# A four-layer graph network kernel: work of the last node stage moved between SP, DVE, ACT and POOL

## The reference

```python
x = _layernorm(x + _L2_gnn_ref(x, ...), axis=-1)
x = _layernorm(x + _L3_gnn_ref(x, ...), axis=-1)   # the last layer
...
# inside _L3_gnn_ref, xs and xv the scalar and vector parts of x:
ssa, sva = fctp_scalar_attr(xs, xv, node_attr, Ws_sc_a, Wv_sc_a)
ssc, svc = fctp_scalar_attr(xs, xv, node_crystal_attr, Ws_sc_c, Wv_sc_c)
s_s, s_v = (ssa + ssc, sva + svc)
...
out_s = C_S * s_s + C_X * o_s      # o_s, o_v: the summed messages, mapped
out_v = C_S * s_v + C_X * o_v
```

## Time and profile before

| what | value |
|---|---|
| median of 3 runs | 3911.85 us (3908.62 to 3913.18) |
| the profiled execution's own time | 3914.43 us |
| its span | 3912.6 us |
| busy share of the span | PE 89%, DVE 69%, ACT 56%, POOL 64% |
| mean granted PE clock | 0.967 of full speed |

### The profile page before, as it was taken

One profiled execution on the slowest core, in us unless ns is written; L12 is line 12 of the kernel. 1 busy time (PEld: TensorE's weight loads), 2 busy tenths in 40 slices (PEclk: granted clock), 3 DMA queues, 4 the chain that ended last, 5 costly groups with the idle time before them and its releaser, 6 DMA issues.

```text
span 3912.6 us, 103757 instructions
## 1 busy us (share of the span) xinstructions
PE 3477.1 (89%) x26652; PEld 3218.3 (82%) x26652; DVE 2710.7 (69%) x10501; ACT 2205.7 (56%) x6014; POOL 2489.7 (64%) x2969
## 2 busy tenths in 40 slices
PE   2799998666599999999979999999989999988886
PEld 2799997565499999877779999877779999987775
DVE  3577775888766666588856666588866666657776
ACT  0244443666544444477745555577756666657777
POOL 1477776888667777566667777400046666658887
PEclk9899998888799999999989999999989999999999
DMA  8622223777522222499822222388832222237775
GB/s 353 248 63 62 61 53 101 255 253 258 180 58 59 57 56 50 118 303 299 287 76 63 61 59 55 93 293 298 297 97 55 53 52 50 45 99 243 239 246 199
DMA packets 424012, 572.02 MB, mean 146 GB/s; under 512 B 218794, under 2 KB 242344, under 8 KB 419590
## 3 DMA queue, kind: packets, MB, share of 16 engines
q1 hardware_dynamic: 280742, 289.28, 25.3%
q10 hardware_dynamic: 61488, 166.57, 10.9%
q0 software_dynamic: 81680, 114.98, 10.8%
HBM read 356.01 MB, written 233.79 MB: 151 GB/s over the span
## 4 chain that ended last, share of the span: by engine, by line
PE 59%; ACT 11%; issue 10%; DVE 7%; DMA 5%; POOL 4%; ACTq 2%; DVEq 1%; POOLq 0%; SPq 0%
PE bank L771 17%; PE bank L804 13%; ACT arena L1049 6%; PE bank L814 5%; PE bank L761 4%; PE bank L827 3%; PE bank L824 3%; PE bank L778 3%; PE bank L819 3%; PE bank L796 3%; ACT same_all L1037 2%; POOL mark_ring L638 2%; DVE stats L1380 2%; ACTq L1020 2%; DVE arena L1373 2%
## 5 line engine op out<-in xcount | busy, mean ns | idle before, releaser
L558 POOL DMA_INDIRECT aggregates<-arena,meta x784 | 790.7, 1008 | 459.7 <-issue 252.1
L771 PE MATMUL bank<-same_all,msg 128*98 (+1 forms) x6272 | 758.6, 275 | 0.0
L545 POOL DMA_INDIRECT xg<-x_after,meta x588 | 585.8, 996 | 252.1 <-issue 247.4
L771 PEld LDWEIGHTS bank<-same_all,msg 128*98 128x98 f32 x6272 | 715.8, 167 | 0.1
L1049 ACT ACTIVATE arena<-arena,shift,rstd 128x160 f32<-128x160 f32 x1500 | 658.4, 513 | 64.1 <-DVE shift L1315 61.5
L961 ACT ACTIVATE w<-bank 1x162 f32<-1x162 f32 (+1 forms) x784 | 257.8, 329 | 741.5 <-PE bank L804 737.6
L804 PE MATMUL bank<-w,arena 98*128 98x32 f32 (+1 forms) x4704 | 628.3, 270 | 0.0
L804 PEld LDWEIGHTS bank<-w,arena 98*128 98x128 f32 x4704 | 590.1, 193 | 0.0
L1380 DVE BATCH_NORM_STATS2 stats<-arena 128x6 f32<-128x160 f32 x1600 | 454.3, 313 | 42.9 <-DVE arena L1373 8.9
L1024 ACT ACTIVATE nT<-bank 128x640 f32<-128x640 f32 x400 | 281.8, 705 | 330.3 <-PE bank L883 179.6
L1268 DVE TENSOR_TENSOR arena<-bank,yv 128x192 f32<-128x192 f32 x294 | 105.1, 358 | 477.9 <-PE bank L824 294.2
(11 more groups left out here) (156 smaller groups left out, 7264.2 us busy)
## 6 DMA issues: line engine op xcount, KB each, us to landing
arena<-aggregates SPq DMA_DIRECT2D x400, 324.0 KB, 4.1
x_after<-arena ACTq DMA_DIRECT2D x300, 320.0 KB, 3.9
arena<-x_after SPq DMA_DIRECT2D x300, 320.0 KB, 3.6
aggregates<-arena ACTq DMA_DIRECT2D x25, 1296.0 KB, 14.7
arena<-nodes SPq DMA_DIRECT2D x100, 320.0 KB, 3.9
out<-arena ACTq DMA_DIRECT2D x100, 320.0 KB, 3.8
same_all<-sorted_dst SPq DMA_DIRECT2D x7, 1792.0 KB, 10.9
aggregates<-arena,meta POOLq DMA_INDIRECT x784, 2.3
```

The source lines that it names most:

```text
L545: gp.indirect_dma_start(xg[:, k % XGR, 4 + t * F:4 + (t + 1) * F], None, xtab[l], at).then_inc(gathered[k], 16)
L558: gp.indirect_dma_start(agg, at, tot[:, kk % TRING, t, 0:AW], None, bounds_check=NP - 1, oob_is_err=False).then_inc(spread[kk], 16)
L771: last = nc.tensor.matmul(bank[5 + t][0:MR, c * P:(c + 1) * P], msg[:, k2, t, c, :], same_all[:, bass.ds(here[t], P)], start=True, stop=True)
```

## The change

All of it is in the node stage of the last layer.

1. The stores of the output leave ACT's list. SP issues them (new L491 in the new file), in iteration b for block b-7 (`OUT_LAG = 7`), ahead of the load of x for block b; SP's iterations run on to 106.
2. DVE's `products` gets a fifth STT: row tile 2, g = 0. It waits for the second `sc_ready` of the block and raises `half_done`.
3. ACT makes three gated halves in place of four: (g, j) = (0, 3), (1, 3), and then (1, 2), the last only once `half_done` says that DVE's fifth STT of the block is done. `half_done` counts three to a block where it counted two.
4. POOL's first addition covers row tile 3 alone (160 columns in place of 320). Its normalization of row tile 3 is gone, and so is the semaphore `last_normed`; ACT normalizes all four row tiles.

```diff
@@ sp: node_loads
+                    if l == 3 and within(b, OUT_LAG, NBLK + OUT_LAG):
+                        kk, tt = back(k, turn, OUT_LAG, NRING)
+                        done = b - OUT_LAG
+                        if not isinstance(b, int):
+                            done = sp.snap(done)
+                        sp.wait_ge(normed, node_count(l, b - OUT_LAG))
+                        alone(sp, passed["sp"])
+                        sp.dma_start(out_rows[bass.ds(done, 1)].rearrange("o p c -> (o p) c"), xn[:, place(kk)]).then_inc(stored[kk], 16)
+                    if not within(b, 0, NBLK):
+                        return
                     if not isinstance(b, int) or b >= X_EARLY:
                         wait(sp, stored[k], node_slot(l, k, turn - 1) * 16)
@@ gpsimd: add_both
-                    if within(b, APPLY_LAG[3], NBLK + APPLY_LAG[3]):
-                        gp.wait_ge(shift_ready, b + (1 - APPLY_LAG[3] + l * NBLK))
-                        alone(gp, passed["gp"])
-                        row = xn[:, place(ka), 3 * F:4 * F]
-                        gp.tensor_scalar(row, row, rstd[:, ka, 3:4], shift[:, ka, 3:4], ALU.mult, ALU.add).then_inc(last_normed, 1)
...
-                        gp.tensor_tensor(x, x, second[:, kk % XGR, 0:2], ALU.add).then_inc(first_added, 1)
+                        gp.tensor_tensor(x[:, 3], x[:, 3], second[:, kk % XGR, 1], ALU.add).then_inc(first_added, 1)
                         gp.wait_ge(first_added, b)
                         alone(gp, passed["gp"])
-                        gp.tensor_tensor(x, x, second[:, kk % XGR, 2:4], ALU.add).then_inc(second_added, 1)
+                        gp.tensor_tensor(x[:, 2:4], x[:, 2:4], second[:, kk % XGR, 2:4], ALU.add).then_inc(second_added, 1)
@@ scalar: node_copies
-                    if within(b, STORE_LAG[l], NBLK + STORE_LAG[l]):
+                    if l < 3 and within(b, STORE_LAG[l], NBLK + STORE_LAG[l]):
...
-                        for g in range(2):
-                            for j in (2, 3):
-                                last = nc.scalar.activation(second[:, kk % XGR, 2 * g + j - 2, :], bank[4 + j][:, g * F:(g + 1) * F],
-                                                            ACT.Copy, scale=attr[:, kk, j, g:g + 1])
+                        for g, j in ((0, 3), (1, 3), (1, 2)):
+                            if j == 2:
+                                act.wait_ge(half_done, b * 3)
+                            last = nc.scalar.activation(second[:, kk % XGR, 2 * g + j - 2, :], bank[4 + j][:, g * F:(g + 1) * F],
+                                                        ACT.Copy, scale=attr[:, kk, j, g:g + 1])
                         last.then_inc(second_gated, 1)
...
-                        for t in range(BT - (l == 3)):
+                        for t in range(BT):
@@ vector: products
+                            dve.wait_ge(sc_ready, base + 2)
+                            row = xn[:, place(k), 2 * F:3 * F]
+                            stt(out=row, in0=bank[6][:, 0:F], scalar=attr[:, k, 2, 0:1], in1=row,
+                                op0=ALU.mult, op1=ALU.add).then_inc(half_done, 1)
                             return
```

More of the change, by code:

```diff
@@ L39 @@
 X_EARLY = 4
+OUT_LAG = 7
 XGR = 4
@@ L331, in build @@
         tot_ready, carried, tot_out = sems("tot_ready", 2), sems("carried", 2), sem("tot_out")
-        last_normed = sem("last_normed")
         half_done = sem("half_done")
@@ L451, in _ @@
                 arows = agg.rearrange("(b p t) c -> b p (t c)", p=P, t=BT)
+                out_rows = out.rearrange("(b p t) c -> b p (t c)", p=P, t=BT)
                 def row_load(b, k):
@@ L488, in node_loads @@
                         aggregate_load(b + A_LEAD[l], (k + A_LEAD[l]) % NRING)
-                steps(sp, 0, NBLK, NODE_STEADY if l else LOADS_STEADY, node_loads, NRING)
+                steps(sp, 0, NBLK + (OUT_LAG if l == 3 else 0), NODE_STEADY if l else LOADS_STEADY, node_loads, NRING)
             for k in range(NRING):
@@ L670, in add_both @@
                     kk, tt = back(k, turn, 1, NRING)
-                    ka, ta = back(k, turn, APPLY_LAG[3], NRING)
-                    if within(b, APPLY_LAG[3], NBLK + APPLY_LAG[3]):
-                        gp.wait_ge(shift_ready, b + (1 - APPLY_LAG[3] + l * NBLK))
-                        alone(gp, passed["gp"])
-                        row = xn[:, place(ka), 3 * F:4 * F]
-                        gp.tensor_scalar(row, row, rstd[:, ka, 3:4], shift[:, ka, 3:4], ALU.mult, ALU.add).then_inc(last_normed, 1)
                     if within(b, 0, NBLK):
@@ L686, in add_both @@
                         alone(gp, passed["gp"])
-                        x = xn[:, place(kk)].rearrange("p (t c) -> p t c", t=BT)[:, 2:4]
-                        gp.tensor_tensor(x, x, second[:, kk % XGR, 0:2], ALU.add).then_inc(first_added, 1)
+                        x = xn[:, place(kk)].rearrange("p (t c) -> p t c", t=BT)
+                        gp.tensor_tensor(x[:, 3], x[:, 3], second[:, kk % XGR, 1], ALU.add).then_inc(first_added, 1)
                         gp.wait_ge(first_added, b)
                         alone(gp, passed["gp"])
-                        gp.tensor_tensor(x, x, second[:, kk % XGR, 2:4], ALU.add).then_inc(second_added, 1)
+                        gp.tensor_tensor(x[:, 2:4], x[:, 2:4], second[:, kk % XGR, 2:4], ALU.add).then_inc(second_added, 1)
                 def node_moves(b, k, turn):
@@ L701, in node_moves @@
                         add_both(b, k, turn)
-                steps(gp, 0, NBLK + (0, NPAIR + XGR - NBLK, 0, APPLY_LAG[3])[l], NODE_STEADY, node_moves, NRING)
+                steps(gp, 0, NBLK + (0, NPAIR + XGR - NBLK, 0, 1)[l], NODE_STEADY, node_moves, NRING)
         @block.tensor
@@ L1005, in sines @@
                                          bias=half_pi[:, :]).then_inc(sin_ready, QUAD)
-                to = out if l == 3 else xtab[l + 1]
-                orows = to.rearrange("(b p t) c -> b p (t c)", p=P, t=BT)
+                orows = xtab[min(l + 1, 3)].rearrange("(b p t) c -> b p (t c)", p=P, t=BT)
                 def node_copies(b, k, turn):
-                    if within(b, STORE_LAG[l], NBLK + STORE_LAG[l]):
+                    if l < 3 and within(b, STORE_LAG[l], NBLK + STORE_LAG[l]):
                         kk, tt = back(k, turn, STORE_LAG[l], NRING)
@@ L1016, in node_copies @@
                         act.wait_ge(normed, node_count(l, b - STORE_LAG[l]))
-                        if l == 3:
-                            act.wait_ge(last_normed, b - (STORE_LAG[3] - 1))
                         alone(act, passed["act"])
@@ L1361, in products @@
                                     if g == 1:
-                                        dve.wait_ge(half_done, b * 2 + (j + 1))
+                                        dve.wait_ge(half_done, b * 3 + (j + 1))
                                     row = xn[:, place(k), j * F:(j + 1) * F]
```

## The result

| | before | after |
|---|---|---|
| median of 5 runs | 3911.85 us (3908.41 to 3913.76) | 3882.37 us (3878.41 to 3884.70) |
| ratio after / before | | 0.9926, interval 0.9911 to 0.9940 |
| the profiled execution's own time; its span | 3914.43; 3912.6 us | 3878.41; 3876.7 us |
| eight blocks of the loop | 32.60 us | 30.44 us |
| a block, mean over blocks 8 to 87 | 4.076 us | 3.806 us |

The medians differ by 29.5 us, 0.75%; 3887 us was forecast for after. The two profiled executions differ by more, 35.9 us of span, since the profiled one of after is its fastest. 8.5 us of that were there before the last node stage began (its first transposes start at 3482.90 before and 3474.42 after), in code that is the same; I put them down to differences between runs, which was not tried by itself. The stage itself went from 429.7 to 402.3 us: 27.4.

A forecast was written before the change was run, and what follows sets the result against it. ACT, never waiting, was taken to set 4.07 us a block, falling to 3.80 under a DVE-ACT ring; 88 x 0.27 = 23.8, plus 1.2 and 0.5, about 25.5 saved, gives 3887 us, range 3879 to 3911.

The forecast's parts named there:

- ACT's issue of the store sets the pace: Last node stage: ACT never waits in its 4.08 us block, 0.83 of it the store issue with its register work.
- POOL's own work: POOL's work in the last node stage: about 3.9 to 4.0 us a block before, about 3.2 after.
- The new ring of 3.76: Once a block: DVE's five STTs, ACT's third half and square root, DVE's reciprocal to next STTs, 3.76 us together.
- The shift comes free: DVE's four-column shift no longer held by POOL's shorter first addition; 0.25 us a block comes off.
- The reading to the letter: A DVE shift held by POOL would then run its whole 0.14, leaving 0.17 of the 0.25 gain: 3894 us.
- The branch back: DVE pays for the loop's branch, formerly covered by ACT: 0.35 us once in eight blocks, 0.04 a block.
- PE's products are never waited for: The block's products end 2.6 us behind the fourth STT, the fifth STT starts 3.7 behind: no wait.
- The sum: 88 loop blocks times 0.27 is 23.8 us, plus 1.2 and 0.5 for written-out blocks: about 25.5 saved.
- The first eight blocks and the drain: Written-out blocks outside the loop: 0.5 us saved in the first eight, 1.2 in five blocks of the drain.
- The very end gains nothing: At the program's end, two normalizations more and one store issue less on ACT: no gain.
- Late x: Rival, chance 0.12: SP's single list delays loads of x beyond 0.3 us of room; 3.9 to 4.15 a block, 3897 to 3919.
- Shift behind L691: Rival, chance 0.06: DVE's shift, issued after POOL's second addition starts, stands until its end; 0.7 a block slower, about 3974.

The follow-up runs named there:

- e1_sp_stores: Kernel before with only the output stores moved from ACT to SP: 3.830 us a block, whole time 0.9972 of before.
- e4_sqrt_first: Changed kernel with ACT's square root ahead of the wait for the fifth STT and the third half: 3.506 us a block, 0.9891 of before.
- e3_pool_320: Changed kernel with POOL's first addition 320 columns wide again: 4.049 us a block, 0.9983 of before.
- e6_shift_in_add: Changed kernel with DVE's shift moved behind the first of the four aggregates, into POOL's second addition: 3.954 us a block.
- e2_no_fifth: Changed kernel without the fifth STT: four halves on ACT, POOL's first addition at 320 columns: 3.819 us a block, 0.9957 of before.
- e8_pool_late: Changed kernel where POOL finally waits for ACT's last normalization and writes one column: 3.811 us a block, end 12.65 us behind the last shift.
- e9_both: Changed kernel with ACT's square root ahead of the wait for the fifth STT and DVE's shift behind the fourth statistic: 3.483 us a block, 0.9897 of before.
- e5_shift_late: Changed kernel with DVE's shift behind the fourth statistic, not the third: 3.739 us a block, 0.9934 of before.

## Why the prediction was right, step by step

- **ACT's issue of the store sets the pace, 0.83 a block.** Right: e1_sp_stores takes it away and nothing else, and the pace falls from 4.076 to 3.830. ACT's time before nT is gone. ACT's own work after the change, 3.39 forecast, is what is left of 3.81 without the 0.41 a block that it waits for the fifth STT (35.9 us over 87 blocks). The step had one size wrong, POOL's own work (3.83 before the change, not 3.9 to 4.0; 3.03 after it, not 3.2); it did not enter the sum.
- **The new ring of 3.76.** Right, to the hundredth, and term by term: five STTs 1.56, ACT wakes 0.03 (3706.47 to 3706.50), third half to square root 0.29 (for 0.27), to reciprocal 0.32 (for 0.36), to the next STTs 1.56 (for 1.55). That ACT's square root ties it is shown by e4_sqrt_first, where the ring opens.
- **The shift comes free, 0.25.** Right: 0.14 for 0.39, and shown by e3_pool_320, which gives back 0.243. The short addition was estimated at 0.58 and takes 0.52; with L693 over at 3707.66, or at 3707.72 had it taken 0.58, and the shift at 3707.78, neither value would have changed the sum. The reading to the letter, which would have given 3894, could not be told from the other by after alone, where the two meet for only 0.02; the held shifts of e3_pool_320 and e6_shift_in_add, which end 0.02 behind POOL, speak against it.
- **The branch back, 0.04 a block.** Right: 30.44 - 8 x 3.76 = 0.36 once in eight blocks, for 0.35.
- **PE's products are never waited for.** Right, though the prediction's own rows give 0.15 + 2.75 = 2.9 and not 2.6 for their end behind the fourth STT; in after it is 2.90 (3706.17 to 3709.07), and the fifth STT comes 3.7 behind.
- **The sum.** The loop: 88 x 0.27 = 23.8 forecast, 23.9 measured (shift of block 8 to shift of block 96). The first eight blocks and the drain: 1.7 forecast, and 0.3 for the start, -0.4 for the first eight and 0.3 for the last three measured, 0.2 in all: that term was nearly nothing. **The very end gains nothing** was wrong: 3.3. The two misses have opposite signs and in part cancel, which is luck: 27.4 against 25.5. The pace, which carries 23.9 of the 27.4, owes nothing to it.
- **Late x.** It cost nothing that shows in after: PE waits for x 9 times in the 87 blocks, 6.1 us in all, and from the second on every eight blocks of the loop take the same 30.43 to 30.44 us (the first take 30.53). The DMA engines were busy 0.76 of the time, no more than before, where the prediction had 0.81; they moved 258 GB/s, for 260. DMA view of after, 3520 to 3850 us (KB, median us to landing):

```profile
out<-arena SPq DMA_DIRECT2D x87, 320.0 KB, 2.2
arena<-x_after SPq DMA_DIRECT2D x87, 320.0 KB, 2.9
```

  Over that stretch stores land in 2.2, where before it is 4.0 from ACT's queue (5.3 in the short stretch of the earlier trace rows). By these medians there are some 3 us more of room than the 0.3 reckoned from the earlier trace rows. In e4_sqrt_first it is used up in some of the blocks.
- **Shift behind L691**, the case on the other side, did not happen; e6_shift_in_add shows that it exists and what a hold of 0.4 costs, 0.15 a block and not the 0.7 of the rival, whose hold would have been longer: DVE is held only for what is left of POOL's instruction, and other gaps run out under the hold.

What the change could have been is the other finding. Its stores alone are worth 0.246 of its 0.270 a block; the fifth STT takes work off ACT and POOL that e2_no_fifth shows not to be needed for 3.82, and it closes a ring. What remained to be had was the order on ACT (e4_sqrt_first, another 0.30).

## What to carry to other kernels

An engine whose row shows gaps may still be the one that sets the pace: count its DMA issues and their register work, here 0.83 of 4.08. When work is moved to a waiting engine, write down the ring that the new wait closes, with every instruction that stands between the two on each engine; its sum gave the new pace, and the order in it (square root before the wait) was worth more than the moved work. And look at which instructions of different engines meet in time: here a DVE instruction of 0.14 us, held by POOL, cost 0.25 a block.

## What was not expected of the hardware

- The program ends 9.4 to 9.5 us behind POOL's last instruction, in all thirteen traces, even where that is a write of one column (e8_pool_late).
- The shift held by POOL ends 0.01 to 0.03 us behind POOL's recorded end, in every block of the loop in before, e1_sp_stores, e2_no_fifth, e3_pool_320, e6_shift_in_add and e9_both; one that was recorded as starting 0.03 behind POOL's addition was not held, and that addition was 0.04 longer (e5_shift_late). Which operands the hold depends on was not tried.
- Held DVE time is partly free: a hold of 0.40 added 0.21 to the stretch from reciprocal to STTs in the block shown, and 0.15 a block to the pace (e6_shift_in_add).
